# A graph convolution whose two edge streams begin with a chunk of 512 columns that stood near their end

## The chip, the cores and the metric

The kernel runs on one core of a Trainium2 chip. The metric is the device time of one execution in microseconds (us). The kernel before took 3414.15 us, the median of three runs (3410.12 to 3417.74). The core has five engines that run side by side and meet at semaphores: PE (TensorE, matrix products), DVE (VectorE), ACT (ScalarE), POOL (GpSimd, here the one that issues gathers) and SP (SyncE, here the one that issues most transfers).

## The reference

A graph network with 3125 nodes, 103125 directed edges (sorted by destination), 64 features and four layers. Each layer computes a softmax-weighted sum over the edges that end in a node:

```python
e   = edge_attr @ enc_edge_w + enc_edge_b
msg = relu(h[src] + e) + 1e-7
m   = msg * t
ex  = exp(m - segment_max(m, dst)[dst])
agg = segment_sum(msg * ex / segment_sum(ex, dst)[dst], dst)
z   = relu(layernorm((h + agg) @ w1 + b1)) @ w2 + b2
```

Between layers there is a residual sum and a layer norm with ReLU; after the last, the input is added and normalised.

## The kernel before, in words

**Streams and chunks.** The sorted edges are cut into two halves, and the second is reversed. Each half lies on 64 partitions (one for each feature) with the edges along the columns, 51712 columns in all (149 of them padding at the front). The columns are worked off in 54 chunks: 49 of 1024 (numbers 0 to 48), then 512, 512, 256, 128, 128. The first 128 columns of chunk 0 are padding and are not gathered. A running maximum, a running denominator and a running numerator go through the columns as scans (lines 938, 953, 969), so that the chunks of a stream must follow each other on DVE. `g = layer * 54 + c` counts the chunks over all layers.

**One chunk, engine by engine.**
- PE multiplies the edge attributes by the encoder (`edge_product`, line 547), into one of four PSUM tiles X. The product of chunk c + 2 is issued after the transposes of chunk c, and waits until the numerator scan of chunk c - 2 has released the tile.
- `h[src]` comes in two ways. POOL gathers rows of `z_table`, 128 edges with one indirect DMA (line 504), and PE transposes them onto X (`add_rows`, line 576). For a chosen chunk only the first 512 columns are gathered, and the second 512 are made on PE by 150 products with one-hot matrices (`add_by_one_hot`, line 566): 60 in part 0 and 90 in part 1, issued around the transposes of the chunks before.
- ACT makes the messages (lines 684, 686), four exponent steps (696 to 701) and the penalties of the next chunk from the bytes `keep` (674). DVE does the running maximum, then the numerator of the chunk before (`numerator_sums`), then the denominator of this one. DVE's first instruction of a chunk is line 936.
- SP stores the rows of each chunk in `rows_table` by four transfers (374), loads attributes (353) and `keep` (364; one block for two chunks, asked for at even chunk numbers, two slots).

**One-hot matrices.** 31 chunks are chosen: 0, 1, and those from 4 to 48 that are even or of the form 8n + 5. In layer 0 the matrices are built by DVE (1033) and ACT (713), used at once for the 29 chunks from 4 on, and stored; those of chunks 0 and 1 are built in slots 50 and 52, for later layers. In layers 1 to 3 they are loaded by ACT's queue (`load_part`, 739), 1.31 MB for part 0 and 1.97 MB for part 1, into two slots: part 0 of the chosen chunk k is used before the transposes of k - 1, and its slot is loaded again from ACT's place in chunk k - 1 (part 0) and k (part 1). Only layers 1 to 3 take chunks 0 and 1 by one-hot.

**Order at the start of a layer.** POOL's gathers wait for the last piece of `z_table`; PE's one-hot products wait for `z_split`, set by DVE's `split_z` (line 998). PE's order is edge products of chunks 0 and 1, then the whole one-hot sum of chunk 0, then the transposes of chunk 0, then the one-hot sum of chunk 1. POOL may be three chunks ahead of PE's transposes. In layer 0, POOL also gathers one piece of keys (line 486) after each of the chunks 1 to 25, and ACT counts it.

Of the kernel before, what the change touches and what calls it, by code (L numbers as in the profile page):

```python
# [4 lines left out]
P = 128  # L5
F = 64
# [6 lines left out]
HALVES = 2  # L13
CH = 1024
KT = CH // P
BANK = 512
SLOTS = 3
XS = 4
SQ = 32
NSQ = CH // SQ  # L20
FB = F // SQ
# [3 lines left out]
COLS = -(-EA // BANK) * BANK  # L25
NBLK = -(-COLS // CH)
TAIL = [512, 512, 256, 128, 128]
WIDTHS = [CH] * ((COLS - sum(TAIL)) // CH) + TAIL
STARTS = [sum(WIDTHS[:_c]) for _c in range(len(WIDTHS))]
NCH = len(WIDTHS)  # L30
# [25 lines left out]
FIRST_CHOSEN = [c for c in range(NCH) if (c % 2 == 0 or c % 8 == 5) and 4 <= c <= 48]  # L56
CHOSEN = [c for c in range(NCH) if c < 2 or (c % 2 == 0 or c % 8 == 5) and 4 <= c <= 48]
BUILD_SLOT = {0: 50, 1: 52}
# [10 lines left out]
def width(c):  # L69
    return WIDTHS[c]  # L70

# [39 lines left out]
def block_of(c):  # L111
    return STARTS[c] // CH, STARTS[c] % CH


def attr_place(c):
    blk, at = block_of(c)
    if width(c) == CH:
        return blk * P, 0, P
    return blk * P + at * HALVES // CH * F, at * HALVES % CH, F
# [19 lines left out]
def gnn_kernel(nc, x_nodes, x_t, dst_stream, src_tiles, src_banks, attr_t, enc_node_w, enc_node_b, enc_edge_w, enc_edge_b,  # L139
# [10 lines left out]
    rows_by_chunk = rows_table[0:BOUNDARY_ROW, :].rearrange("(c b i h) (f e) -> c (h f) i b e", c=NBLK, i=SQ, h=HALVES, f=FB)  # L150

    with ExitStack() as ctx:
# [180 lines left out]
        def _(sp):  # L333
# [33 lines left out]
            def store_rows(layer, c, parts):  # L367
                g = layer * NCH + c
                blk, at = block_of(c)
                b0 = at // SQ  # L370
                n = NSQ - b0 if layer == 0 and c == NCH - 1 else width(c) // SQ
                sp.wait_ge(rows_ready, g + 1)
                for a in parts:
                    sp.dma_start(rows_by_chunk[blk, a, :, b0:b0 + n, :],  # L374
                                 rows[g % 2][a * SQ:(a + 1) * SQ, 0:n].rearrange("i b q j -> i b (q j)")).then_inc(stored[g % 2], 16)
# [288 lines left out]
        def _(act):  # L664
# [122 lines left out]
            for layer in range(LAYERS):  # L787
# [33 lines left out]
                blk, at = block_of(c)  # L821
                b0 = at // SQ
                n = NSQ - b0 if layer == 0 else width(c) // SQ
                for a in range(NSTORE // 2, NSTORE):
                    act.dma_start(rows_by_chunk[blk, a, :, b0:b0 + n, :],
                                  rows[g % 2][a * SQ:(a + 1) * SQ, 0:n].rearrange("i b q j -> i b (q j)")).then_inc(stored[g % 2], 16)
# [438 lines left out]
```

## Time and profile before

| what | value |
|---|---|
| median of 3 runs | 3414.15 us |
| profiled execution, its own time | 3407.53 us |
| its span, first to last instruction | 3405.7 us |
| mean granted TensorE clock | 0.876 |
| DVE busy | 2874.5 us (84%) |
| POOL busy (0.3 us of issue before each gather not counted) | 2310.8 us (68%) |
| DMA, mean busy share of the 16 engines | 88.8% in queues q1, q10 and q0 together |

Layer 0's stream begins on DVE at 54 us, those of layers 1, 2 and 3 at 1020, 1819 and 2620 us. Between the last chunk of a layer and the first of the next lie the node stage and the start of the stream, 96 to 99 us. A row of the timeline gives start, duration, engine, line, operation, count, and in brackets how long the engine sat idle before and what released it.

### The profile page before, as it was taken

The numbers are of one execution on the slowest core, as the hardware profiler recorded it, in microseconds if no ns is written. First come the engines' busy times: TensorE is split into PE (matmuls) and PEld (weight loads), VectorE is DVE, ScalarE is ACT, GpSimd is POOL, SyncE is SP. The second block draws the span as 40 slices with busy tenths as digits, with TensorE's granted clock in tenths as the row PEclk, the third lists the DMA queues.
The fourth block names the chain that finished last, engine by engine and source line by source line (L and its number), as shares of the span: only waits on it lengthen the run. The fifth ranks groups of instructions, "written<-read, shape, count | busy, mean of one in ns | idle before, by whom it ended". The sixth has DMA issues, their size and how long they took to land.

```text
span 3405.7 us, 55091 instructions
## 1 busy us (share of the span) xinstructions
PE 2695.8 (79%) x21852; PEld 1361.5 (40%) x21852; DVE 2874.5 (84%) x2835; ACT 1782.3 (52%) x2240; POOL 2310.8 (68%) x2381
## 2 busy tenths in 40 slices
PE   2778877888279888988748899889938988899854
PEld 1334333334144444444333444444415444444423
DVE  6899999999857888898976888888875889888895
ACT  2777775666424544455443544545543445444554
POOL 5777776676257777777627777777735777777742
PEclk9889988889669999999858999999957999999975
DMA  5999999999838999999847999999964999999971
GB/s 147 282 273 311 304 289 259 272 289 287 231 117 269 287 304 302 295 295 297 215 122 219 305 292 306 283 298 309 276 154 136 294 292 294 305 298 300 280 187 39
DMA packets 1047266, 878.26 MB, mean 258 GB/s; under 512 B 911066, under 2 KB 937183, under 8 KB 1015200
## 3 DMA queue, kind: packets, MB, share of 16 engines
q1 hardware_dynamic: 940912, 478.76, 54.8%
q10 hardware_dynamic: 28960, 305.28, 23.8%
q0 software_dynamic: 77136, 90.71, 10.2%
q8 instruction: 171, 2.80, 0.3%
q14 instruction: 87, 0.71, 0.1%
HBM read 555.79 MB, written 318.70 MB: 257 GB/s over the span
## 4 chain that ended last, share of the span: by engine, by line
DVE 34%; PE 16%; SPq 15%; issue 9%; POOL 9%; DMA 8%; ACT 8%; DVEq 0%; ACTq 0%; POOLq 0%
PE X L566 13%; SPq L374 9%; POOL gath L504 8%; DVE decay L938 7%; DMA keep<-keep_dram 6%; DVE state_all L969 6%; DVE one_hot L1033 5%; DVE rows_all L924 4%; SPq L364 4%; DVE X L943 4%; DVE state_all L953 3%; ACT X L686 2%; ACT msg L684 2%; SPq L353 1%; PE X L547 1%
## 5 line engine op out<-in xcount | busy, mean ns | idle before, releaser
L504 POOL DMA_INDIRECT gath<-z_table,idx x2248 | 2189.6, 974 | 862.5 <-issue 694.3
L566 PE MATMUL X<-one_hot,z_parts 128*64 128x512 fp8e5 x11550 | 1352.1, 396 | 149.2 <-DVE one_hot L1033 124.5
L566 PEld LDWEIGHTS X<-one_hot,z_parts 128*64 128x64 bf16 x11550 | 666.9, 114 | 870.8 <-DVE one_hot L1033 162.3
L566 PE MATMUL X<-between,z_parts 128*64 128x512 fp8e5 x6750 | 763.2, 386 | 2.8 <-DMA between<-one_hot_dram 2.8
L696 ACT ACTIVATE decay<-X 128x1024 f32<-128x1024 f32 (+2 forms) x216 | 209.3, 969 | 927.5 <-DVE X L943 923.2
L566 PEld LDWEIGHTS X<-between,z_parts 128*64 128x64 bf16 x6750 | 380.8, 112 | 394.6 <-issue 72.1
L924 DVE STREAM_TRANSPOSE rows_all<-state_all 128x1024 f32<-128x1024 f32 (+3 forms) x432 | 505.9, 1171 | 8.4 <-DMA rows_table<-rows_all 1.0
L547 PE MATMUL X<-attr,enc_edge 64*64 64x512 f32 (+1 forms) x1648 | 268.5, 703 | 306.8 <-DVE state_all L969 297.4
L953 DVE TENSOR_TENSOR_SCAN state_all<-decay,state_all,X 128x1024 f32<-128x1024 f32 (+2 forms) x216 | 468.2, 2168 | 20.0 <-ACT X L701 20.0
L938 DVE TENSOR_TENSOR_SCAN decay<-X,decay 128x1023 f32<-128x1023 f32 (+2 forms) x216 | 477.2, 2209 | 7.7
L969 DVE TENSOR_TENSOR_SCAN state_all<-decay,state_all,X 128x1024 f32<-128x1024 f32 (+2 forms) x216 | 468.1, 2167 | 0.0
L684 ACT ACTIVATE msg<-X,edge_bias 128x1024 f32<-128x1024 f32 (+2 forms) x216 | 226.1, 1047 | 278.2 <-PE X L576 278.2
L936 DVE TENSOR_TENSOR decay<-decay,top 128x1 f32<-128x1 f32 x216 | 34.2, 158 | 351.7 <-ACT X L686 338.0
L674 ACT ACTIVATE decay<-keep 128x1024 f32<-128x1024 uint8 (+2 forms) x216 | 213.7, 990 | 223.4 <-DMA keep<-keep_dram 223.4
L956 DVE SCALAR_TENSOR_TENSOR X<-msg,X 128x1024 f32<-128x1024 f32 (+2 forms) x216 | 250.4, 1159 | 7.5
L943 DVE TENSOR_TENSOR X<-X,decay 128x1024 f32<-128x1024 f32 (+2 forms) x216 | 250.0, 1157 | 0.0
L576 PE MATMUL X<-ident,gath 128*128 128x128 f32 x1128 | 180.9, 296 | 80.9 <-DMA gath<-z_table,idx 80.7
L686 ACT ACTIVATE X<-msg,tcol 128x1024 f32<-128x1024 f32 (+2 forms) x216 | 229.6, 1063 | 7.0
L519 POOL DMA_INDIRECT between<-rows_table,pos_i x100 | 95.0, 950 | 180.3 <-DMA rows_table<-ends_row 104.4
L699 ACT ACTIVATE decay<-decay 128x1024 f32<-128x1024 f32 (+2 forms) x216 | 213.1, 987 | 0.0
L697 ACT ACTIVATE X<-X 128x1024 f32<-128x1024 f32 (+2 forms) x216 | 208.1, 963 | 0.0
L701 ACT ACTIVATE X<-X 128x1024 f32<-128x1024 f32 (+2 forms) x216 | 207.1, 959 | 0.0
(160 smaller groups left out, 1458.0 us busy)
## 6 DMA issues: line engine op xcount, KB each, us to landing
rows_table<-rows_all SPq DMA_DIRECT2D x784, 256.0 KB
attr<-attr_t SPq DMA_DIRECT2D x196, 512.0 KB
one_hot<-one_hot_dram ACTq DMA_DIRECT2D x48, 1920.0 KB
between<-one_hot_dram ACTq DMA_DIRECT2D x45, 1920.0 KB
one_hot<-one_hot_dram ACTq DMA_DIRECT2D x48, 1280.0 KB
one_hot_dram<-one_hot SPq DMA_DIRECT2D x31, 1920.0 KB
between<-one_hot_dram ACTq DMA_DIRECT2D x45, 1280.0 KB
one_hot_dram<-one_hot SPq DMA_DIRECT2D x31, 1280.0 KB
```

Source lines behind the costliest of these rows:

```text
L374: sp.dma_start(rows_by_chunk[blk, a, :, b0:b0 + n, :], rows[g % 2][a * SQ:(a + 1) * SQ, 0:n].rearrange("i b q j -> i b (q j)")).then_inc(s ...
L504: pool.indirect_dma_start(out=gath[s][:, n * F:(n + 1) * F], out_offset=None, in_=z_table, in_offset=bass.IndirectOffsetOnAxis(ap=idx[:, c ...
L547: last = nc.tensor.matmul(X[g % XS][h * F:(h + 1) * F, b * BANK:b * BANK + w], enc_edge2[b * F:(b + 1) * F, :], attr[s][b * F:(b + 1) * F, ...
L566: last = nc.tensor.matmul(x[h * F:(h + 1) * F, BANK:CH], z_parts[:, i * GB + k, third, :], bank[:, i, k, h * BANK:(h + 1) * BANK], start=F ...
L684: nc.scalar.activation(msg[s][:, 0:w], X[g % XS][:, 0:w], ACT.Relu, bias=edge_bias[:, :]).then_inc(msg_ready, 1)
L686: nc.scalar.activation(X[g % XS][:, 0:w], msg[s][:, 0:w], ACT.Copy, scale=tcol[:, layer:layer + 1])\
L924: v.transpose(rows[g % 2][:, 0:w // SQ, q, :], state[g % 2][:, q, 0:w].rearrange("p (b j) -> p b j", j=SQ))\
L938: v.tensor_tensor_scan(out=m[:, 1:w], data0=x[:, 0:w - 1], data1=m[:, 1:w], initial=m[:, 0:1], op0=ALU.max, op1=ALU.add).then_inc(run_max, 1)
L943: v.tensor_tensor(x, x, m, ALU.subtract).then_inc(shifted, 1)
L953: v.tensor_tensor_scan(out=state[g % 2][:, 0, 0:w], data0=decay[s][:, 0:w], data1=X[g % XS][:, 0:w], initial=state[(g - 1) % 2][:, 0, befo ...
L956: v.scalar_tensor_tensor(out=X[g % XS][:, 0:w], in0=msg[s][:, 0:w], scalar=EPS_MSG, in1=X[g % XS][:, 0:w], op0=ALU.add, op1=ALU.mult).then ...
L969: v.tensor_tensor_scan(out=state[g % 2][:, 1, 0:w], data0=decay[s][:, 0:w], data1=X[g % XS][:, 0:w], initial=state[(g - 1) % 2][:, 1, befo ...
```

## The change

The widths become 512, then 49 times 1024, then 512, 256, 128, 128: still 54 chunks and the same columns. Chunk 0 has 512 columns and no one-hot part in any layer. The chosen chunks become 1, 2, and those from 5 to 49 that are odd or of the form 8n + 6; the two that only later layers use are built in slots 51 and 53. The chunks of 1024 keep their order of chosen and not chosen, each with a number higher by one. What goes by the number itself does not move: `keep` is asked for at even numbers (its first block is now 1536 columns), keys are gathered after chunks 1 to 25, and `load_part` has its place by rules on c. Since a chunk no longer lies within one block of 1024, rows are stored by squares of 32 columns at the same addresses as before, and each chunk's attributes get rows of their own.

```diff
-TAIL = [512, 512, 256, 128, 128]
-WIDTHS = [CH] * ((COLS - sum(TAIL)) // CH) + TAIL
+HEAD = [512]
+TAIL = [512, 256, 128, 128]
+WIDTHS = HEAD + [CH] * ((COLS - sum(HEAD + TAIL)) // CH) + TAIL
...
-FIRST_CHOSEN = [c for c in range(NCH) if (c % 2 == 0 or c % 8 == 5) and 4 <= c <= 48]
-CHOSEN = [c for c in range(NCH) if c < 2 or (c % 2 == 0 or c % 8 == 5) and 4 <= c <= 48]
-BUILD_SLOT = {0: 50, 1: 52}
+FIRST_CHOSEN = [c for c in range(NCH) if (c % 2 == 1 or c % 8 == 6) and 5 <= c <= 49]
+CHOSEN = [1, 2] + FIRST_CHOSEN
+BUILD_SLOT = {1: 51, 2: 53}
...
-def block_of(c):
-    return STARTS[c] // CH, STARTS[c] % CH
+ATTR_PARTS = [P if w > BANK else F for w in WIDTHS]
...
 def attr_place(c):
-    blk, at = block_of(c)
-    if width(c) == CH:
-        return blk * P, 0, P
-    return blk * P + at * HALVES // CH * F, at * HALVES % CH, F
+    return sum(ATTR_PARTS[:c]), 0, ATTR_PARTS[c]
...
-    rows_by_chunk = rows_table[0:BOUNDARY_ROW, :].rearrange("(c b i h) (f e) -> c (h f) i b e", c=NBLK, i=SQ, h=HALVES, f=FB)
+    rows_by_square = rows_table[0:BOUNDARY_ROW, :].rearrange("(b i h) (f e) -> (h f) i b e", i=SQ, h=HALVES, f=FB)
...
-                b0 = at // SQ
-                n = NSQ - b0 if layer == 0 and c == NCH - 1 else width(c) // SQ
+                b0 = STARTS[c] // SQ
+                n = NBLK * NSQ - b0 if layer == 0 and c == NCH - 1 else width(c) // SQ
...
-                    sp.dma_start(rows_by_chunk[blk, a, :, b0:b0 + n, :],
+                    sp.dma_start(rows_by_square[a, :, b0:b0 + n, :],
```

PE at the start of layer 1 (after the node stage), before: the products of two chunks, then all 150 one-hot products of chunk 0 ahead of its transposes (x4), then the 150 of chunk 1.

```order
L547 MATMUL X<-attr,enc_edge 64x512 x8
L566 MATMUL X<-one_hot,z_parts 64x512 x150
L576 MATMUL X<-ident,gath 128x128 x4
L566 MATMUL X<-between,z_parts 64x512 x150
L547 MATMUL X<-attr,enc_edge 64x512 x4
L576 MATMUL X<-ident,gath 128x128 x4
L547 MATMUL X<-attr,enc_edge 64x512 x4
L576 MATMUL X<-ident,gath 128x128 x8
L547 MATMUL X<-attr,enc_edge 64x512 x4
L566 MATMUL X<-one_hot,z_parts 64x512 x60
L576 MATMUL X<-ident,gath 128x128 x8
L566 MATMUL X<-one_hot,z_parts 64x512 x90
```

The same place in the changed kernel (its line numbers are 4 lower):

```order
L543 MATMUL X<-attr,enc_edge 64x512 x6
L572 MATMUL X<-ident,gath 128x128 x4
L562 MATMUL X<-one_hot,z_parts 64x512 x150
L543 MATMUL X<-attr,enc_edge 64x512 x4
L562 MATMUL X<-between,z_parts 64x512 x60
L572 MATMUL X<-ident,gath 128x128 x4
L562 MATMUL X<-between,z_parts 64x512 x90
L543 MATMUL X<-attr,enc_edge 64x512 x4
L572 MATMUL X<-ident,gath 128x128 x4
L543 MATMUL X<-attr,enc_edge 64x512 x4
L572 MATMUL X<-ident,gath 128x128 x8
L543 MATMUL X<-attr,enc_edge 64x512 x4
```

Chunk 0's transposes now stand ahead of all one-hot products. Between the transposes of chunks 0 and 1 stand 150 + 60 one-hot products where 150 stood, since chunk 2 is chosen too.

ACT at the start of layer 1 (loads of one-hot matrices; 128x2560 is part 0, 128x3840 part 1), before:

```order
L674 ACTIVATE decay<-keep 128x1024
L739 DMA between<-one_hot_dram 128x2560
L739 DMA between<-one_hot_dram 128x3840
L684 ACTIVATE msg<-X,edge_bias 128x1024
L686 ACTIVATE X<-msg,tcol 128x1024
L739 DMA one_hot<-one_hot_dram 128x2560
L739 DMA one_hot<-one_hot_dram 128x3840
L696 ACTIVATE decay<-X 128x1024
L697 ACTIVATE X<-X 128x1024
```

And in the changed kernel:

```order
L670 ACTIVATE decay<-keep 128x512
L735 DMA between<-one_hot_dram 128x2560
L735 DMA between<-one_hot_dram 128x3840
L680 ACTIVATE msg<-X,edge_bias 128x512
L682 ACTIVATE X<-msg,tcol 128x512
L692 ACTIVATE decay<-X 128x512
L693 ACTIVATE X<-X 128x512
L695 ACT_TABLE_LOAD
L695 ACTIVATE decay<-decay 128x512
L697 ACTIVATE X<-X 128x512
L670 ACTIVATE decay<-keep 128x1024
L680 ACTIVATE msg<-X,edge_bias 128x1024
```

The third matrix is no longer loaded within chunk 0; its load stands behind the messages of chunk 1.

## Rows read from the trace of the kernel before

**Rows 1.** Waits of all engines: engine line, released by: us, times, longest

```profile
DVE decay L936 <- ACT X L686: 338.0, 96, 22.3
...
ACT decay L674 <- DMA keep<-keep_dram: 223.4, 67, 7.6
...
POOL between L519 <- DMA rows_table<-rows_all: 46.6, 1, 46.6
```

**Rows 2.** Windows of 20 us, layer 1: PE, PEld, DVE, ACT, POOL busy; PEclk, DMA share, GB/s

```profile
990.00:1010.00 20.00, 12.29 (x94) 5.74 (x92) 7.91 (x5) 0.00 (x0) 14.82 (x14) 0.68 0.72 252
...
1210.00:1230.00 20.00, 20.00 (x180) 9.98 (x178) 19.79 (x16) 12.93 (x14) 15.09 (x16) 1.00 1.05 348
```

**Rows 3.** Timeline of PE at the start of layer 1

```profile
998.10 18.72 PE L566 MATMUL X<-one_hot,z_parts 128*64 128x512 fp8e5 x150 [7.71 <-DVE z_parts L998]
...
1034.67 0.66 PE L576 MATMUL X<-ident,gath 128*128 128x128 f32 x4
...
1045.18 1.99 PE L547 MATMUL X<-attr,enc_edge 64*64 64x512 f32 x8 [7.81 <-DVE state_all L969]
1047.09 8.41 PE L566 MATMUL X<-one_hot,z_parts 128*64 128x512 fp8e5 x60
1055.44 1.09 PE L576 MATMUL X<-ident,gath 128*128 128x128 f32 x8
1066.29 1.09 PE L547 MATMUL X<-attr,enc_edge 64*64 64x512 f32 x8
1067.31 6.67 PE L566 MATMUL X<-between,z_parts 128*64 128x512 fp8e5 x60
```

**Rows 4.** Timeline of POOL, layer 1: gathers number 1, 6 and 46

```profile
991.22 0.94 POOL L504 DMA_INDIRECT gath<-z_table,idx  x1 [27.58 <-DMA z_table<-z_sb]
...
999.16 0.95 POOL L504 DMA_INDIRECT gath<-z_table,idx  x1 [0.30 <-issue]
...
1050.48 0.94 POOL L504 DMA_INDIRECT gath<-z_table,idx  x1 [0.30 <-issue]
```

**Rows 5.** Timeline of DVE, layer 1: first instructions of chunks 0, 1, 2, 4, 22 and 44

```profile
1019.75 0.16 DVE L936 TENSOR_TENSOR decay<-decay,top 128x1 f32<-128x1 f32 x1 [21.70 <-ACT X L686]
...
1037.72 0.16 DVE L936 TENSOR_TENSOR decay<-decay,top 128x1 f32<-128x1 f32 x1 [3.35 <-issue]
...
1049.71 0.15 DVE L936 TENSOR_TENSOR decay<-decay,top 128x1 f32<-128x1 f32 x1
...
1076.90 0.16 DVE L936 TENSOR_TENSOR decay<-decay,top 128x1 f32<-128x1 f32 x1 [3.07 <-ACT X L686]
...
1333.01 0.16 DVE L936 TENSOR_TENSOR decay<-decay,top 128x1 f32<-128x1 f32 x1 [6.23 <-ACT X L686]
...
1633.35 0.16 DVE L936 TENSOR_TENSOR decay<-decay,top 128x1 f32<-128x1 f32 x1 [1.67 <-ACT X L686]
```

**Rows 6.** Timeline of DVE, end of layer 1: first instructions of chunks 50 and 51

```profile
1708.17 0.15 DVE L936 TENSOR_TENSOR decay<-decay,top 128x1 f32<-128x1 f32 x1
...
1714.83 0.15 DVE L936 TENSOR_TENSOR decay<-decay,top 128x1 f32<-128x1 f32 x1
```

**Rows 7.** Timeline of POOL and PE, layer 0: last gather and transposes of chunks 0, 1

```profile
39.55 0.94 POOL L504 DMA_INDIRECT gath<-z_table,idx  x1 [0.30 <-issue]
42.04 1.97 PE L576 MATMUL X<-ident,gath 128*128 128x128 f32 x8 [10.74 <-DMA gath<-z_table,idx]
...
63.11 0.94 POOL L504 DMA_INDIRECT gath<-z_table,idx  x1 [0.30 <-issue]
...
70.44 1.97 PE L576 MATMUL X<-ident,gath 128*128 128x128 f32 x8 [24.53 <-DMA gath<-z_table,idx]
```

**Rows 8.** Layer 0, start: last gathers of chunks 3 and 4; DVE's chunk 3

```profile
107.51 1.10 POOL L504 DMA_INDIRECT gath<-z_table,idx  x1 [0.30 <-issue]
...
119.37 0.94 POOL L504 DMA_INDIRECT gath<-z_table,idx  x1 [0.30 <-issue]
...
115.71 0.16 DVE L936 TENSOR_TENSOR decay<-decay,top 128x1 f32<-128x1 f32 x1 [3.71 <-ACT X L686]
```

**Rows 9.** Layer 0: DVE's first instruction of chunk 26

```profile
503.52 0.16 DVE L936 TENSOR_TENSOR decay<-decay,top 128x1 f32<-128x1 f32 x1 [1.28 <-ACT X L686]
```

More of the change, by code:

```diff
@@ L368, in store_rows @@
                 g = layer * NCH + c
-                blk, at = block_of(c)
-                b0 = at // SQ
-                n = NSQ - b0 if layer == 0 and c == NCH - 1 else width(c) // SQ
+                b0 = STARTS[c] // SQ
+                n = NBLK * NSQ - b0 if layer == 0 and c == NCH - 1 else width(c) // SQ
                 sp.wait_ge(rows_ready, g + 1)
                 for a in parts:
-                    sp.dma_start(rows_by_chunk[blk, a, :, b0:b0 + n, :],
+                    sp.dma_start(rows_by_square[a, :, b0:b0 + n, :],
                                  rows[g % 2][a * SQ:(a + 1) * SQ, 0:n].rearrange("i b q j -> i b (q j)")).then_inc(stored[g % 2], 16)
@@ L820, in _ @@
                 act.wait_ge(rows_ready, g + 1)
-                blk, at = block_of(c)
-                b0 = at // SQ
-                n = NSQ - b0 if layer == 0 else width(c) // SQ
+                b0 = STARTS[c] // SQ
+                n = NBLK * NSQ - b0 if layer == 0 else width(c) // SQ
                 for a in range(NSTORE // 2, NSTORE):
-                    act.dma_start(rows_by_chunk[blk, a, :, b0:b0 + n, :],
+                    act.dma_start(rows_by_square[a, :, b0:b0 + n, :],
                                   rows[g % 2][a * SQ:(a + 1) * SQ, 0:n].rearrange("i b q j -> i b (q j)")).then_inc(stored[g % 2], 16)
@@ L1218 @@
     src_s = chunked(streams(src, 0)).transpose(3, 1, 2, 0).reshape(P, NBLK * KT * HALVES)
-    src_b = np.stack([streams(src, 0)[:, c * CH + BANK:(c + 1) * CH] for c in BANKS]).reshape(P, SUB)
+    src_b = np.stack([streams(src, 0)[:, STARTS[c] + BANK:STARTS[c] + CH] for c in BANKS]).reshape(P, SUB)
     attr_h = streams(attr, 0)
-    attr_s = np.zeros((NBLK * P, CH), attr.dtype)
+    attr_s = np.zeros((sum(ATTR_PARTS), CH), attr.dtype)
     for c in range(NCH):
```

## The prediction, as it was put on record before the changed kernel ran

> **What bounds the kernel now.** I read the table of waits first, then DVE's timeline for the first instruction of every chunk (line 936), then PE and POOL at the places where those starts are late, then the windows for the DMA share.
>
> DVE is the engine through which all columns must go, and the profiled execution leaves it 338.0 us of idle time ahead of line 936 [rows 1]. Its chunk starts show three stages in each of the layers 1 to 3.
>
> - *Front.* The stream of layer 1 starts at 1019.75, after 21.70 us of idling [rows 5]: PE had put 150 one-hot products of chunk 0 (18.72 us) ahead of its transposes. Chunk 1 starts 18 us later, after 150 more. In that time POOL gathers without a pause, 1.25 us apart (from number 6 at 999.16 to number 46 at 1050.48, 40 steps in 51.3 us [rows 4]).
> - *Middle.* A chunk costs DVE 12.0 us of work (chunk 1 to 2, without a gap, 1037.72 to 1049.71), 96 for eight. But from chunk 4 (1076.90) to chunk 44 (1633.35) are 556.45 us [rows 5], 111.3 for eight chunks. Read the same way, layers 2 and 3 give 111.3 and 111.4. The DMA share is 1.05 in a window there, against 0.72 at the front [rows 2], so I take the transfers (rows out, one-hot matrices, `keep` in) as what paces the middle. Where a chunk is late, it is mostly an even one, whose `keep` bytes came late: 223.4 us of ACT's time in 67 waits [rows 1]; or one behind one-hot sums of neighbouring chosen chunks.
> - *Tail.* After the last loads DVE runs without a gap. The interval from chunk 50 to 51 (512 columns) is 1714.83 - 1708.17 = 6.66 us [rows 6].
>
> Layer 0 differs: until chunk 4 POOL's gathers bound it (DVE's chunk 3 waits 3.71 us [rows 8]), later DVE itself, which also builds matrices.
>
> **The method.** The full chunks keep their order, each with its number raised by one. So I set new chunk k + 1 against old chunk k. The change is then a delay of this pairing at the front, less one chunk of 512 at the tail. The work in all is the same: as many gathers, products and scans.
>
> **Layers 1 to 3, front.** New chunk 0 needs only six gathers. The sixth is issued at 999.16 [rows 4], and I take 4 us until it lands. The bounds for this: in layer 0 the transposes begin 42.04 - 39.55 = 2.5 us after the last gather of chunk 0, and 70.44 - 63.11 = 7.3 us after that of chunk 1, with loads under way [rows 7]; number 46 had landed at most 5.0 us after its issue (1050.48 against 1055.44) [rows 3, 4].
>
> The sum in times of layer 1:
> - landed 1003.2, transposes 0.7, then PE's 150 products of chunk 1 at 18.7 (first ones of the layer, as before), edge product 1.1, 60 products of chunk 2 at 6.7, transposes 0.7 [rows 3]: chunk 1 is ready at 1031.1.
> - DVE starts 2.4 us after the transposes end (1034.67 + 0.66 to 1037.72 [rows 3, 5]): new chunk 1 at 1033.5. Its cycle is about 11.6, as ACT's exponents are late behind a short numerator; PE's 90 products, 1.5 times 6.7, and what goes with them give the same: new chunk 2 at 1045.1.
> - The numerator that frees the tile for the edge product of new chunk 5 comes 7.5 us later (1037.72 to 1045.18 in the old pair), at 1052.6. The old one was at 1045.18 [rows 3]: a delay of 7.4.
> - Then PE does 2.0 + 8.4 us (1063.0) and needs number 54, issued 8 steps of 1.25 after 1050.48, at 1060.5, and landed at 1064.5. That is 1.5 more: 9 us.
>
> The early start of DVE, 1006 instead of 1020, thus buys only half a chunk. The next full chunk waits for PE, which now has 210 one-hot products between the first two transposes [PE's order above], and later for POOL, which has eight gathers more ahead of each paired chunk, 8 x 1.25 = 10 us. The delay is 5.9 with a landing of 2.5 us (no wait for number 54), and 12.6 with 7.3 (10.7, and then 1.9 at number 54).
>
> At a landing of 4 us it stands that the six gathers pass the 3.28 MB of one-hot matrices that ACT asks for at 998. In the Trainium skill (DMA: Bandwidth & Descriptors, Queues, rings and completion order) each DMA engine "round-robins between the queue rows it has work for", packet by packet, so that a small gather shares the engines with a big load and needn't wait for its end. The 5.0 us at most of number 46 agree, though its window was not full. By service in order of issue instead, it would land some 11 us after its issue (3.28 MB at about 300 GB/s, between the 252 and 348 of [rows 2]), and the delay would be 13 to 16. I keep 9.
>
> **Layers 1 to 3, middle.** Per eight chunks the bytes are the same, so the paired delay is carried through, if the DMA engines pace this stage. What does change is the phase: `keep` is still asked for at even numbers, and the chosen chunks are now odd. I cost this at nothing, since another order doesn't take work away from a full queue, and bound it by the two mechanisms below, -27 and +31 us in all.
>
> ACT loads the third matrix behind the messages of new chunk 1 (about 1034 instead of 1018.65 for old chunk 0). It is used at 1055; 1.31 + 1.31 MB at half of 300 GB/s take 17 us. Just in time; 2 us at worst, in the upper bound.
>
> **Layers 1 to 3, tail.** One interval of 6.66 us falls away [rows 6]. POOL has then only a few gathers left and is ahead of DVE, so that its own shift is hidden. Per layer 9 - 6.7 = +2.3 (from -0.8 to +5.9, and +8 with the late matrix); for three +7 (-2 to +24).
>
> **Layer 0.** Old chunk 3 waits for the gather issued at 107.51. New chunk 4 also needs eight gathers and a piece of keys more, those that end the stretch at 119.37 [rows 8]: +11.9, and DVE, which had waited 3.71, could not have been earlier by itself (new chunk 3 is bound by gathers in the same way). Chunk 0 doesn't matter, since the gathers after it bind. Back come 6.7 at the tail, where DVE is the bound (its matrix building moves along with its chunks), and 1.3 from old chunk 26, which waited for ACT's count of keys [rows 9]: the keys stop at number 25, one chunk earlier in the pairing. But the last built matrix is now stored within the last 400 columns; POOL waits here for the last rows (46.6 us in all, once [rows 1]), and 1.97 MB at 300 GB/s are 6.6 us, most of which overlaps. I take 1 of them. Together +5 (+3.9 to +10).
>
> The edits of addresses (attributes, squares) change neither counts nor sizes of transfers: nothing.
>
> **Sum.** 5 + 7 = +12. The profiled execution took 3407.53 us, 1.8 more than its span, and would take 3419.5. It lies 6.6 below the median of the runs shown, 3414.15; on the scale of the medians the forecast is 3426 us. Its own range, from +2 to +34 without the phase, is 3416 to 3448.
>
> **Rivals.**
> - *The phase helps (faster).* At each group of three neighbouring chosen chunks PE makes the second one late by about 6 us (6.7 + 10.0 for its products and 1.8 for the rest [rows 3], against 12.0). Its number is now even, so that the `keep` wait falls into the same gap. Before, it came one chunk later: chunk 22 waits 6.23 us [rows 5], and the six such chunks of a layer some 18. If half of it really goes, 9 us in each of three layers, -27 + 12 = -15: 3399. It decides once it gives back over 4 us a layer. Against it: the cycle of eight takes 111.3 in three layers alike, although its waits lie elsewhere each time.
> - *The phase hurts.* The load that runs beside the fetch of `keep` is now part 1, 1.97 MB, where it was part 0, 1.31: 0.66 MB at 300 GB/s, 2.2 us. With 19 plain even chunks in each of three layers and a quarter of it exposed, +31: 3457. For it speaks that `keep` is what ends most waits; against it again the full queues, and that the rows before it then go out faster.
> - *Front and tail cancel (no change).* The gathers land after 2.5 us, layer 0 stays at +4: in all about +2, 3416.
> - *Nothing lands in time.* First gathers behind the load, 13 to 16 of delay, +4 to +7 more a layer: 3438 to 3447, inside the range.
>
> **How the numbers follow.** The forecast with its own range gets 0.48, with its lowest part (under +6.8) counted as no change; the phase that helps 0.20, mostly faster; the phase that hurts 0.12; the cancelling 0.15; the late landing 0.05. About 0.2%, 6.8 us, is what a measurement of this kernel tells from no change. Slower: 0.12 + 0.05 + 0.40 of the forecast = 0.57. Same: 0.15 + 0.08 + 0.02 of the helping phase = 0.25. Faster: 0.18. The range reaches to both phases in part: 3402 to 3452. The likeliest case's own range stands above.
>
> **What would show it.** In the trace of the changed kernel, layer 1 counted from its first gather (991.2 before):
> - first instruction of DVE 15 us after it, not 28.5; chunk 1 at 42 (old chunk 0 at 28.5), chunk 5 at about 94.7 (old chunk 4 at 85.7). If chunk 5 comes at 91 or less, the front is cheaper than I say.
> - DVE without a gap from chunk 49 on, and 6.7 us less for it.
> - eight chunks of the middle in 111.3 us. Under 110 or over 112.5 the phase matters, and I am wrong about what paces it; the waits of ACT for `keep` say which way.
> - layer 0: chunk 4 at 127.6, not old chunk 3's 115.7, and the last chunk some 4 us later than before.
> - the same count of instructions, gathers and bytes. If not, the pairing fails.

## The result, and the profile after

| kernel | median | range | runs |
|---|---|---|---|
| before, beside it | 3412.3 us | 3410.1 to 3417.7 | 4 |
| changed | 3486.7 us | 3481.2 to 3492.5 | 4 |

The ratio is 1.0211 (95% interval 1.0189 to 1.0233): the change costs 74 us where +12 was forecast, and the time lies 35 us above the range. The profiled execution took 3490.05 us, 1.9 more than its span, against 3407.53: +82.5.

The table of waits of the changed kernel answers to [rows 1] (engine line, released by: total, times, longest):

```profile
DVE decay L931 <- ACT X L682: 369.1, 85, 10.5
ACT decay L670 <- DMA keep<-keep_dram: 361.8, 67, 10.8
...
POOL gath L500 <- PE X L572: 164.0, 75, 17.6
```

ACT still waits 67 times for `keep`, but 361.8 us where it was 223.4. POOL's line of the same table before was:

```profile
POOL gath L504 <- PE X L576: 90.4, 44, 12.8
```

The amount of work is unchanged, as the first lines of the page show (55091 instructions, DVE 2874.6 us busy as against 2874.5), with the same packets and bytes:

```profile
span 3488.2 us, 55091 instructions
...
DMA packets 1047266, 878.26 MB, mean 252 GB/s; under 512 B 911066, under 2 KB 937183, under 8 KB 1015200
```

The front of layer 1. POOL's first and sixth gather, PE's first transposes, and DVE's first instructions of chunks 0, 1, 2 and 5, from the timeline of the changed kernel (start, duration, engine, line), which answer to [rows 3 to 5]:

```profile
995.39 0.94 POOL L500 DMA_INDIRECT gath<-z_table,idx  x1 [27.43 <-DMA z_table<-z_sb]
...
1003.34 0.94 POOL L500 DMA_INDIRECT gath<-z_table,idx  x1 [0.30 <-issue]
...
1009.84 1.11 PE L572 MATMUL X<-ident,gath 128*128 128x128 f32 x4 [15.29 <-DMA gath<-z_table,idx]
```

```profile
1012.44 0.16 DVE L931 TENSOR_TENSOR decay<-decay,top 128x1 f32<-128x1 f32 x1 [10.22 <-ACT X L682]
1039.08 0.16 DVE L931 TENSOR_TENSOR decay<-decay,top 128x1 f32<-128x1 f32 x1 [16.91 <-issue]
1050.48 0.15 DVE L931 TENSOR_TENSOR decay<-decay,top 128x1 f32<-128x1 f32 x1
...
1090.87 0.16 DVE L931 TENSOR_TENSOR decay<-decay,top 128x1 f32<-128x1 f32 x1 [4.29 <-ACT X L682]
```

Chunk 5 starts 1090.87 - 995.39 = 95.5 us after the first gather. Old chunk 4 started after 85.7: the front costs 9.8 us, and 9 was forecast. In layers 2 and 3 it costs 9.9 and 8.5.

The middle of layer 1. DVE's first instructions of chunks 14 to 19 and of chunk 45:

```profile
1224.94 0.16 DVE L931 TENSOR_TENSOR decay<-decay,top 128x1 f32<-128x1 f32 x1 [9.19 <-ACT X L682]
1236.93 0.15 DVE L931 TENSOR_TENSOR decay<-decay,top 128x1 f32<-128x1 f32 x1
1254.73 0.16 DVE L931 TENSOR_TENSOR decay<-decay,top 128x1 f32<-128x1 f32 x1 [5.72 <-ACT X L682]
1266.73 0.18 DVE L931 TENSOR_TENSOR decay<-decay,top 128x1 f32<-128x1 f32 x1
1282.29 0.16 DVE L931 TENSOR_TENSOR decay<-decay,top 128x1 f32<-128x1 f32 x1 [3.45 <-ACT X L682]
1294.28 0.15 DVE L931 TENSOR_TENSOR decay<-decay,top 128x1 f32<-128x1 f32 x1
...
1671.70 0.15 DVE L931 TENSOR_TENSOR decay<-decay,top 128x1 f32<-128x1 f32 x1
```

Only every second chunk waits, and it is the even one, for which `keep` is fetched. From chunk 5 to 45 are 580.83 us, 116.2 for eight chunks; layers 2 and 3 give 115.0 and 115.9. Before it was 111.3, 111.3 and 111.4. The differences of 4.9, 3.7 and 4.5, five cycles in each layer, make 66 us. Read by the pairing of the prediction (new chunk k + 1 against old chunk k), the delay grows from 13.97 to 38.35 us between chunk 5 and chunk 45 of layer 1. With the chunks up to 49 the growth comes to 25, 20 and 25 us in the three layers, 70 in all.

The rest went much as forecast. The time from the start of the last full chunk of layer 1 (old 48, new 49) to that of the last chunk is 35.7 us before and 29.1 after: 6.6 back. Layer 0 ends 2.95 us later (DVE's last chunk at 923.35 instead of 920.40), and the next layer's first gather comes 995.39 - 991.22 = 4.2 later. The three fronts cost 28.3 us and the three tails give back 19.6; with the 4.2 and the 70 that makes 83, and 82.5 were measured.

How the fetch and the wait follow each other is seen on SP's queue and ACT, at the even chunk that starts at 1254.73. SP (SPq is its issuing of transfers), in the changed kernel:

```profile
1263.36 7.23 SPq L370 DMA_DIRECT2D rows_table<-rows_all  x4
1270.62 4.32 SPq L361 DMA_DIRECT2D keep<-keep_dram  x2
```

And ACT at that place:

```profile
1264.65 0.33 ACTq L735 DMA_DIRECT2D one_hot<-one_hot_dram  x1
...
1279.04 1.06 ACT L670 ACTIVATE decay<-keep 128x1024 f32<-128x1024 uint8 x1 [4.44 <-DMA keep<-keep_dram]
```

The same place before, old chunk 16, which started at 1246.77, on SP and on ACT:

```profile
1255.39 6.44 SPq L374 DMA_DIRECT2D rows_table<-rows_all  x4
1261.87 4.14 SPq L364 DMA_DIRECT2D keep<-keep_dram  x2
```

```profile
1256.69 0.33 ACTq L739 DMA_DIRECT2D between<-one_hot_dram  x1
...
1269.41 1.06 ACT L674 ACTIVATE decay<-keep 128x1024 f32<-128x1024 uint8 x1 [2.81 <-DMA keep<-keep_dram]
```

SP asks for `keep` behind four row stores, ACT has asked for a one-hot part 5 to 6 us earlier, and the penalties wait for `keep`. Both loads stand in ACT's place in chunk 17. In the changed kernel, where 17 is chosen, it is a part 1 (1.97 MB); before, where 18 is chosen, it was a part 0 (1.31 MB). Over the plain even chunks of layers 1 to 3 (those followed by one without a wait), `keep` is used 9.0 us after its request in the changed kernel and 7.7 before. The request itself comes 16.2 us after the start of the chunk instead of 15.2. The mean of all 63 pairs of chunks rose from 27.55 to 28.71 us, and 63 x 1.16 = 73 us.

### The profile page after: what moved, and what is told of

Same layout as the page of the kernel before. It is cut to its first block, busy times and chain, and to the rows that moved or that the text cites. A ratio compares the mean times of both kernels' runs of the same rounds, so it can differ in the third digit from the quotient of the medians.

```text
span 3488.2 us, 55091 instructions
## 1 busy us (share of the span) xinstructions
PE 2696.8 (77%) x21852; PEld 1361.6 (39%) x21852; DVE 2874.6 (82%) x2835; ACT 1781.7 (51%) x2240; POOL 2309.7 (66%) x2381
## 4 chain that ended last, share of the span: by engine, by line
DVE 34%; SPq 19%; DMA 10%; ACT 10%; issue 9%; PE 9%; POOL 9%; DVEq 0%; ACTq 0%; POOLq 0%
SPq L370 12%; POOL gath L500 9%; DVE decay L933 7%; DMA keep<-keep_dram 7%; PE X L562 7%; SPq L361 7%; DVE state_all L964 6%; DVE rows_all L919 5%; DVE one_hot L1028 5%; DVE X L938 4%; DVE state_all L948 2%; ACT X L682 2%; ACT msg L680 2%; ACT x_sb L709 1%; ACT between L709 1%
## 5 line engine op out<-in xcount | busy, mean ns | idle before, releaser
L670 ACT ACTIVATE decay<-keep 128x1024 f32<-128x1024 uint8 (+2 forms) x216 | 213.8, 990 | 361.9 <-DMA keep<-keep_dram 361.8
L680 ACT ACTIVATE msg<-X,edge_bias 128x1024 f32<-128x1024 f32 (+2 forms) x216 | 226.0, 1046 | 204.0 <-PE X L572 203.9
L515 POOL DMA_INDIRECT between<-rows_table,pos_i x100 | 95.1, 951 | 203.0 <-DMA rows_table<-ends_row 120.8
L572 PEld LDWEIGHTS X<-ident,gath 128*128 128x128 f32 x1128 | 127.0, 147 | 247.4 <-DMA gath<-z_table,idx 146.0
L543 PEld LDWEIGHTS X<-attr,enc_edge 64*64 64x64 f32 x1648 | 52.8, 149 | 428.6 <-issue 407.0
```

The costliest lines, as they stand in the source:

```text
L543: last = nc.tensor.matmul(X[g % XS][h * F:(h + 1) * F, b * BANK:b * BANK + w], enc_edge2[b * F:(b + 1) * F, :], attr[s][b * F:(b + 1) * F, ...
L572: last = nc.tensor.matmul(X[g % XS][:, k * P:(k + 1) * P], gath[s][:, k * P:(k + 1) * P], ident[:, :], is_transpose=True, start=False, sto ...
L680: nc.scalar.activation(msg[s][:, 0:w], X[g % XS][:, 0:w], ACT.Relu, bias=edge_bias[:, :]).then_inc(msg_ready, 1)
```

## The experiments

The theory after the result: the lost 70 us are the wait for `keep`, which the move by one number has set beside the larger part. The place of the request for `keep` in the pattern of chosen and unchosen chunks is called its phase here. The rival is that the DMA queues as a whole are the pace and `keep` only shows it. Each time is set against runs of the kernel before on the same chip; intervals are of 95%.

### The phase of `keep`, and `keep` out of the way

In `a_keep_odd` and `b_keep_odd` the blocks of `keep` begin at odd chunk numbers, in the changed kernel and in the one before. That gives the changed kernel the old neighbourhood back, and the old kernel the new one. (The first block is a single chunk then, NKEEP is 26 in both, and a block is asked for at the first chunk of the block before.)

```diff
-    return min(c // KEEP_CHUNKS, NKEEP - 1)
+    return min((c + 1) // KEEP_CHUNKS, NKEEP - 1)
...
-    return range(b * KEEP_CHUNKS, (b + 1) * KEEP_CHUNKS if b < NKEEP - 1 else NCH)
+    return range(max(b * KEEP_CHUNKS - 1, 0), (b + 1) * KEEP_CHUNKS - 1 if b < NKEEP - 1 else NCH)
...
```

> The changed kernel, with the keep blocks moved by one chunk: block 0 is chunk 0 alone, then chunks (1,2), (3,4) and so on, so that keep is asked for at odd numbers, in the same place against the chosen chunks as before the change. Theory P (the phase of keep against the chosen chunks cost the 70 us of the middle): the cycle of eight goes back from 115.7 to 111.4 us, ACT's waits for keep from 362 to about 225 us, and the time to about 3425 (3415 to 3435), what the prediction had without the phase. Rival W (the first chunk of 512 and the order of one-hot loads at the front disturb the stream, and keep is only where it shows): the time stays within 15 us of 3487.

> The kernel before, with the same move of the keep blocks: asked for at odd numbers while the chosen chunks are even. Theory P: it becomes slower by what the changed kernel lost in the middle, to about 3480 (3465 to 3495), cycle of eight 115 to 116, all of DVE's waits at odd numbers. Rival W: no more than 15 us slower.

In `a_keep3` and `b_keep3` there are three slots, and each block is asked for one block earlier.

```diff
-KEEP_SLOTS = 2
+KEEP_SLOTS = 3
...
```

> The changed kernel with three slots for keep, each block asked for two chunks (some 27 us) earlier. Theory P: no wait for keep is left (under 40 us of ACT's time), and the middle falls at least to 111.4 per eight chunks: 3425 or less. If the DMA engines pace the middle, as the prediction had it, the cycle then stays at 111 to 112 and other waits take the place; if keep's way (rows stored, keep issued, landed) paced it, the cycle falls to what PE allows, about 100 to 104, and the time to 3370 or less.

> The kernel before with three slots for keep. If the DMA engines paced its middle (prediction): within 10 us of 3412, cycle 111. If it was paced by keep: the cycle falls to 100 to 105 and the time to 3310 to 3370.

Measured, beside 3415.4 us of the kernel before:

| run | median | ratio (interval) | eight chunks, layers 1, 2, 3 | ACT waits for `keep` |
|---|---|---|---|---|
| a_keep_odd | 3442.8 | 1.0084 (1.0062 to 1.0106) | 112.3, 112.8, 113.1 | 262.7 |
| b_keep_odd | 3476.1 | 1.0183 (1.0162 to 1.0204) | 114.9, 114.6, 116.3 | 368.7 |
| a_keep3 | 3413.3 | 0.9987 (0.9973 to 1.0000) | 110.4, 110.8, 110.8 | 3.8 |
| b_keep3 | 3398.7 | 0.9948 (0.9928 to 0.9968) | 111.1, 110.3, 111.1 | 4.0 |

The kernel before, with nothing changed but the phase, loses 61 us and waits for `keep` as long as the changed one. The changed kernel, with the phase put back, recovers 47 of its 74 us: 27.4 us are left against the runs beside it. That is less than expected (3415 to 3435 us, a cycle of 111.4), and what the other part is was not tested. With a third slot the wait is gone, and the two kernels have the same cycle, 110.3 to 111.1 us. So the phase of `keep` is the cause of the loss in the middle. What remains of the change is 3413.3 - 3398.7 = 14.6 us, where the prediction had +12 for front, tail and layer 0. The two traces show it there: 6.8 us at layer 1's first gather (996.71 against 989.96), 26.1 lost at the three fronts, 19.5 given back at the three tails, and in the middle no more than 1.5 us, in sum over the three layers. `b_keep3` fell between its two expectations: the cycle stayed at 111, but the time is 17 us lower.

### What paces the middle without the wait

Both runs start from `b_keep3`. In `b_k3_gath14`, POOL makes 14 gathers instead of 16 for each full unchosen chunk of layers 1 to 3 (its loop runs to `issued_tiles`), so that the last 128 columns of such a chunk lack `h[src]` in both streams. In `b_k3_halfhot`, the loads of one-hot matrices bring only 64 of the 128 partitions from the third chosen chunk of a layer on, and the rest keeps older values.

```diff
+def issued_tiles(layer, c):
+    n = gathered_tiles(layer, c)
+    return n - 1 if layer > 0 and n == KT else n
...
-                    for n in range(first_tile(c) * HALVES, gathered_tiles(layer, c) * HALVES):
+                    for n in range(first_tile(c) * HALVES, issued_tiles(layer, c) * HALVES):
```

> The kernel before with three keep slots, and 14 instead of 16 gathers for each full chunk that isn't chosen, in layers 1 to 3 (the last 128 columns of both halves keep old data). Eight chunks then need 82 gathers and not 88. Theory G (with keep out of the way, POOL's gathers, one each 1.25 us, pace the middle: 88 x 1.249 = 109.9, measured 110.3 to 111.1): the cycle falls to 103 to 104.5, layers 1 to 3 get 35 to 45 us shorter each, the time about 3280 (3265 to 3305). Theory D (the DMA engines pace it, as the prediction said): the gathers are a tenth of the DMA time, 6 of 88 of them under 1% of it, so the cycle stays over 109 and the time over 3380.

```diff
-                act.dma_start(hot[j % HOT_SLOTS][:, a:b].bitcast(f32), one_hot_dram[n * P:(n + 1) * P, a:b].bitcast(f32))\
+                full = P if j < HOT_SLOTS else P // 2
+                act.dma_start(hot[j % HOT_SLOTS][0:full, a:b].bitcast(f32), one_hot_dram[n * P:n * P + full, a:b].bitcast(f32))\
```

> The kernel before with three keep slots, and only half of the bytes (64 of 128 partitions) of each one-hot load from the third on in layers 1 to 3; the other half keeps old data, all instructions stay. Theory G: cycle 110 as before, within 0.5 us (POOL's 88 gathers), time within 12 us of 3399. Theory D: 2 x 31 loads carry 23% of the DMA time, half of it goes, the cycle falls by 10 or more to what DVE and PE allow, 100, and the time to 3300 or less.

Measured, beside 3418.9 us of the kernel before: `b_k3_gath14` 3350.9 us, ratio 0.9797 (0.9775 to 0.9820), eight chunks in 108.5, 107.9 and 107.2 us; `b_k3_halfhot` 3404.5 us, ratio 0.9955 (0.9941 to 0.9970), eight chunks in 110.7, 111.0 and 111.3.

Two windows of 400 us in layers 1 and 2 show both (columns as in [rows 2]). First `b_keep3`:

```profile
1100.00:1500.00 400.00, 360.73 (x3038) 176.44 (x3036) 350.50 (x265) 206.05 (x208) 302.23 (x321) 0.94 1.02 300
1900.00:2300.00 400.00, 355.44 (x3038) 175.18 (x3036) 349.45 (x265) 205.59 (x207) 302.45 (x321) 0.96 1.02 300
```

Then `b_k3_halfhot`:

```profile
1100.00:1500.00 400.00, 362.25 (x3062) 176.33 (x3058) 350.47 (x267) 205.74 (x208) 302.31 (x321) 0.94 1.02 226
1900.00:2300.00 400.00, 360.46 (x3052) 176.17 (x3050) 351.05 (x267) 207.42 (x209) 302.47 (x321) 0.95 1.01 226
```

A quarter less data per second doesn't shorten the time or the cycle, and leaves the busy share of the DMA engines as it was: they aren't the pace. POOL is, with 321 gathers in 400 us in each row, 1.246 us from one to the next. A cycle of eight chunks has 88 gathers, and 88 x 1.249 = 109.9 us, against 110.3 to 111.1 measured. In `b_k3_gath14` a cycle has 6 gathers fewer (three of eight chunks are unchosen), and it falls by 3 us and not by the 7.5 that POOL alone would give. I had expected 3265 to 3305 us, so the next limit is nearer than I thought. The waits of this run name it. DVE's waits before its chunks fall from 13.7 us a cycle in `b_keep3` to 7.4, and another one comes up:

```profile
DVE rows_all L929 <- DMA rows_table<-rows_all: 67.3, 30, 7.4
```

DVE waits there until rows of an earlier chunk have been stored. In `b_keep3` this took 5.4 us in all; here it is 4.4 us in each cycle of eight. So the stores of rows, which are DMA, stand close behind POOL.

The changed kernel has POOL waiting instead, as its windows show:

```profile
1100.00:1500.00 400.00, 342.02 (x2924) 166.71 (x2922) 322.15 (x244) 189.07 (x191) 294.79 (x314) 0.93 0.97 284
1900.00:2300.00 400.00, 359.62 (x3078) 175.67 (x3076) 330.48 (x252) 192.46 (x194) 296.80 (x315) 0.94 0.99 289
```

And the kernel before in the same windows:

```profile
1100.00:1500.00 400.00, 355.25 (x3044) 173.52 (x3042) 344.45 (x262) 201.38 (x203) 302.15 (x322) 0.95 1.02 298
1900.00:2300.00 400.00, 358.89 (x3042) 174.59 (x3040) 343.64 (x261) 200.63 (x202) 302.45 (x321) 0.94 1.00 296
```

POOL's 321 or 322 gathers are its full pace. Before, the waits for `keep` were nearly hidden under it (a cycle of 111.3 us against 109.9); in the changed kernel they aren't any more.

### How much of the phase is the size of the part beside `keep`

`SPLIT = 3` cuts the one-hot matrices the other way round: part 0 has 1.97 MB, part 1 has 1.31.

```diff
-SPLIT = 2
+SPLIT = 3
```

> The kernel before with the one-hot parts cut 3 + 2 and not 2 + 3 pieces: part 0 is then 1.97 MB and part 1 1.31 MB, so that the larger part is loaded beside the fetch of keep, as in the changed kernel, with all chunk numbers and sizes as before. Theory S (the size of the part beside the keep fetch makes the phase dear): slower by 30 to 70 us, cycle 113.5 to 116, ACT's waits for keep over 300 us. Rival R (it is not the load's size, but where the row stores and the PE waits of the neighbouring chosen chunks fall against keep): within 15 us of 3415, keep waits 200 to 250.

> The changed kernel with the same cut, 3 + 2 pieces: the smaller part, 1.31 MB, now loads beside the fetch of keep. Theory S: most of the loss of the middle comes back, 3425 to 3450, cycle 111.5 to 113, keep waits under 280 us. Rival R: within 15 us of 3487.

> The kernel before with keep asked for at odd numbers and the one-hot parts cut 3 + 2: both changes together, so that the smaller part loads beside the keep fetch again. If the size of that part explains the whole of the phase: back to 3410 to 3425, cycle 111.5. If it explains a part, as the two cuts so far suggest (b_split3 37 us slower, a_split3 14 faster): 3440 to 3465, cycle 113 to 114.

`b_split3` took 3455.9 us beside 3418.9, ratio 1.0101 (1.0076 to 1.0126); `a_split3` 3473.1, ratio 1.0146 (1.0115 to 1.0176); `b_odd_split3`, which has the odd blocks too, 3437.7, ratio 1.0059 (1.0036 to 1.0082), beside 3417.1. On the kernel before this makes a square of differences (us) from the runs beside each:

| `keep` asked for in | smaller part beside it | larger part beside it | the size (other cut) alone |
|---|---|---|---|
| a chosen chunk (as before) | 0 | +37 | +37 |
| an unchosen chunk (as after) | +21 | +61 | +40 |
| this neighbourhood alone | +21 | +24 | |

Each entry has an interval of some 8 us either way. Within it the two causes add up, and the size of the neighbouring load is the larger one. The spans of the traces, one execution of each, give +50, +64 and +27 instead, so that the adding up isn't shown more closely than that. The other cut also sets 90 products ahead of the transposes where 60 stood. On the kernel before this isn't what costs: in a cycle of eight, ACT's waits for `keep` grow from 12.9 to 16.8 us and DVE's before its chunks from 14.9 to 18.8, while ACT's waits for PE stay (6.8 and 6.4). Over the whole kernel ACT waits 279.1 us for `keep` in `b_split3`, where I had expected over 300. `b_odd_split3` came out 2 us below the 3440 to 3465 expected for a part of the phase.

The landing of `keep` moves with the size: it is used 7.7 us after its request before and 9.6 in `b_split3`; 9.0 in `b_keep_odd` and 8.0 in `b_odd_split3`. The cause of the other 21 to 24 us is not shown. The trace says where they are: in `b_odd_split3` DVE's waits before the first two chunks of a group of three neighbouring chosen ones are 9.6 us a cycle instead of 7.5, and before the other six chunks 7.2 instead of 7.4.

On the changed kernel the same cut gives back only 14 us (20 against the runs beside each), by cycles of 113.1 to 114.7 instead of 115.0 to 116.2. This lies in the band of the rival, not in that of the theory (3425 to 3450). Its waits are:

```profile
ACT msg L680 <- PE X L572: 359.9, 65, 21.6
...
ACT decay L670 <- DMA keep<-keep_dram: 213.2, 61, 7.8
```

The wait for `keep` is below that of the kernel before (223.4 us), so here it isn't what is left of the loss; ACT waits 359.9 us for PE, where it was 203.9 in the changed kernel. The shorter cycles are worth 29 us, but the three fronts lose 17.6: chunk 5 comes 101.3, 100.3 and 101.3 us after the first gather, instead of 95.5, 94.7 and 95.1. Between the first two transposes stand 240 one-hot products there, where 210 stood.

### `keep` ahead of the row stores

The same two slots, but SP asks for the next block just before it stores the rows of the odd chunk, not after (and at chunk 0 of the later layers).

```diff
-                    if c % KEEP_CHUNKS == 0 and c // KEEP_CHUNKS < NKEEP - 1 and layer * NKEEP + c // KEEP_CHUNKS >= 1:
-                        load_keep(layer * NKEEP + c // KEEP_CHUNKS + KEEP_SLOTS - 1)
+                    if c == 0 and layer > 0:
+                        load_keep(layer * NKEEP + KEEP_SLOTS - 1)
...
+                    if (c + 1) % KEEP_CHUNKS == 0 and (c + 1) // KEEP_CHUNKS < NKEEP - 1:
+                        load_keep(layer * NKEEP + (c + 1) // KEEP_CHUNKS + KEEP_SLOTS - 1)
                     store_rows(layer, c, range(FB))
```

> The changed kernel with two keep slots, but SP asks for keep ahead of the four row stores it stood behind. Theory Q (what makes keep late is its place in SP's queue: it starts some 16 us after the chunk's start, behind the rows of the chunk before, and lands 9 us later): ACT's waits for keep fall below 80 us, the cycle to 110.5 to 111.5 (POOL's gathers), the time to 3405 to 3425, as with three slots. If the row stores only take its place in the queue and come late themselves: over 3440, with DVE waiting for stored rows.

> The kernel before with the same move of the request. Theory Q: 3395 to 3405, as with three slots, so that the two kernels are again 10 to 16 us apart (the front's price less the tail's return).

Beside 3417.1 us: `a_keep_early` 3416.2, ratio 0.9997 (0.9983 to 1.0011); `b_keep_early` 3398.1, ratio 0.9938 (0.9915 to 0.9961). ACT waits 22.3 and 16.2 us for `keep`, and the cycles are 110.1 to 110.8 in both. This is SP in `a_keep_early`:

```profile
1254.64 1.10 SPq L361 DMA_DIRECT2D keep<-keep_dram  x2
1255.79 11.11 SPq L370 DMA_DIRECT2D rows_table<-rows_all  x4
```

And ACT, whose penalties have no wait in brackets:

```profile
1266.55 1.04 ACT L672 ACTIVATE decay<-keep 128x1024 f32<-128x1024 uint8 x1
```

The two requests take 1.10 us to issue here, against 4.32 behind the stores. As a mean over layers 1 to 3 it is 1.6 us, against 4.1 before and 4.9 in the changed kernel. The stores behind them take longer in return (1.94 us each as a mean, 1.50 in the changed kernel), but DVE waits only 7.2 us in all for stored rows. With the same bytes and the same slots, the order on SP's queue alone takes the wait away: `keep` is late because it stands behind the rows. This makes the fastest kernel of the study, without a further slot, level with `b_keep3`, and 0.6% faster than the kernel before. `a_keep_early` and `b_keep_early` both fell into what was expected.

### What the last 15 us are

`a_even` has the changed widths with the chosen chunks at their old numbers, one place earlier in the pairing. POOL then has eight gathers fewer ahead of each paired chunk.

```diff
-FIRST_CHOSEN = [c for c in range(NCH) if (c % 2 == 1 or c % 8 == 6) and 5 <= c <= 49]
+FIRST_CHOSEN = [c for c in range(NCH) if (c % 2 == 0 or c % 8 == 5) and 4 <= c <= 48]
...
-BUILD_SLOT = {1: 51, 2: 53}
+BUILD_SLOT = {1: 50, 2: 52}
```

> The changed widths (512 first) with the chosen chunks at their old numbers (even or 8n + 5, from 4 to 48, and 1 and 2), so that the phase against keep is restored by moving the chosen chunks and not keep. Theory P: cycle 111.3 to 112.8 and keep waits of 220 to 270 us as in a_keep_odd; the time 3420 to 3450. If the loss lay in the sizes and not in the phase: over 3465.

It took 3422.7 us, ratio 1.0012 (0.9996 to 1.0027): no difference from the kernel before can be told. Its cycles are 112.8, 111.4 and 111.1, and ACT waits 246.4 us for `keep`. It differs from `a_keep_odd` (3442.8, the same neighbourhood of `keep`) by POOL's lead and by the place of the pattern. The traces put 8.4 us of the difference into layer 0, where the first gather of layer 1 comes at 987.45 us instead of 995.85, and the rest into the layers behind it. This speaks for the lead as what costs, also in the middle, but doesn't separate it.

`a_even_early` puts the edit of `a_keep_early` on top of it, to find out whether the 15 to 18 us between the two kernels are POOL's lead or PE's order at the front. The same program was measured three times, once with `b_keep_early` beside it (`b_keep_early2`).

> The changed kernel with the chosen chunks at their old numbers (1, 2, and from 4 on the even ones or of the form 8n + 5) and keep asked for ahead of the row stores. Without waits for keep the middle goes at POOL's pace, and the changed kernel was still 18 us behind the old one (3416.2 against 3398.1). Theory (POOL's lead): what is left is the eight gathers, 8 x 1.25 = 10 us, that POOL makes more than before ahead of each paired full chunk; with the chosen chunks one number earlier in the pairing these eight are gone, and each of the four layers gives back 3 to 6 us: 3392 to 3404, cycle of eight still 110 to 111. Rival (front on PE): what is left is the 210 one-hot products between the first two transposes and the ready times behind them; the pattern doesn't touch that, and the time stays at 3412 to 3420.

> The same kernel as a_even_early once more (its first run, and the kernel before beside it, took 4585 and 4615 us, which is another pace of the whole chip than in all other runs). Lead theory: 3392 to 3404, cycle of eight 110 to 111. Rival, the front on PE: 3412 to 3420.

> The kernel before with keep asked for ahead of the row stores, again, on the same chip as a_even_early2, so that the two can be set side by side: 3396 to 3400. Lead theory: within 5 us of a_even_early2. Rival: 14 or more under it.

> The same kernel as a_even_early once more, hoping for the pace of the first twelve runs. If the kernel before takes about 3415 beside it: lead theory (POOL's eight gathers are what is left), ratio 0.993 to 0.997 (3392 to 3404), cycle of eight 110 to 111. Rival, the front on PE: ratio 0.999 to 1.002 (3412 to 3420). If the kernel before again takes some 4600, the question stays open.

In all these runs every kernel took a third longer, the kernel before too: 4614.9, 4618.0 and 4695.0 us. The runs gave 4585.4 (ratio 0.9935, 0.9913 to 0.9956), 4591.3 (0.9943, 0.9927 to 0.9960) and 4686.7 (0.9981, 0.9965 to 0.9998); `b_keep_early2` 4614.2 (0.9983, 0.9968 to 0.9998), 23 us above `a_even_early2` beside it, which neither theory had expected. The waits of the first of them show that another engine is the bound there:

```profile
PEld X L564 <- issue: 1380.9, 2030, 5.9
DVE decay L933 <- ACT X L684: 1190.9, 155, 22.5
...
POOL gath L502 <- PE X L574: 945.7, 119, 19.4
```

POOL waits 945.7 us for PE, and PE has long stretches of "issue", in which nothing in the profile holds it. POOL's lead can decide nothing there, so these four runs say nothing on the question at the usual pace, and it stays open.

## Why the prediction was wrong

**The direction and the parts outside the middle were right.** The front was put at 9 us and cost 9.8 in layer 1 (9.9 and 8.5 in the others), with chunk 5 at 95.5 us after the first gather instead of 94.7. The gathers landed 6.5 us after the issue of the sixth (1003.34 to 1009.84), not 4, near the upper of my two bounds; that made chunk 0 start at 17.1 us and not 15. By my own sum it should have delayed chunk 5 by 11.4 us in all, so that the 9 came out in part by luck. The sum has a slip too: PE's time and the landing of number 54 move together, so its 1.5 us stay at every landing, and the bounds are 7.4 and 12.2, not 5.9 and 12.6. Neither matters against what was missed. The tail gave back 6.6 of the 6.66 forecast. In layer 0, chunk 4 came at 126.69 (forecast 127.6), and 4.2 us were left at the next layer's first gather (forecast 5). With the wait for `keep` out of the way in both kernels, the change costs 14.6 us (third slot) or 18.1 (earlier request), where the sum said 12.

**The step that failed is the phase of `keep`,** "I cost this at nothing, since another order doesn't take work away from a full queue". It cost 70 us of 82.5 in the two profiled executions, and 60 of 74 by the medians (74.4 less the 14.6 that are left with a third slot). Two things were wrong in it.

- *The pace of the middle was taken from a busy share.* A DMA share of 1.05 [rows 2] was read as a full queue. `b_k3_halfhot` moves 226 GB/s instead of 300 at the same share of 1.02 and in the same time. The pace was POOL's chain of gathers, 88 x 1.249 = 109.9 us for eight chunks. The row for it stood in front of me: 16 gathers in 20 us in the window 1210 to 1230 of [rows 2] is 1.25 us for each, POOL without a pause. The page hides it, since it counts 0.94 us of each gather as busy and gives POOL 68%.
- *So the wait for `keep` wasn't bound to a pace that would absorb it.* It was nearly hidden under POOL's pace (a cycle of 111.3 against 110.3 to 111.1 without it), and a lengthening came out almost in full: 3.9 us more of it in a cycle made the cycle 3.4 longer (`b_split3`). The rival "the phase hurts" had the right mechanism, the larger load beside the fetch. But I priced it with a quarter exposed, +31. Measured are 37 to 40 us for the other cut and 21 to 24 for the rest of the phase on the kernel before, and 70 in the changed one. Near full exposure (57 chunks x 2.2 us = 125 us at most) should have been the upper end. Moreover the stage from which `keep` is late is SP's queue, four stores ahead of it, and I didn't look there.

**The other rivals.** "The phase helps" was false in its sign: PE's wait and that for `keep` do fall on the same chunk now (even chunks wait 94.7 us in the five cycles of layer 1, odd ones 0.3; before 50.8 and 23.5), but their sum grew. Front and tail don't cancel: they leave 28.3 - 19.6 = 8.7 us in the three layers. A late landing of the first gathers was not seen; 6.5 us is less than the 11 that service in order of issue would give.

**My own test pointed the right way.** I had written that over 112.5 us for eight chunks the phase matters and I am wrong about what paces the middle. It came out at 115.0 to 116.2.

## What to carry to other kernels

A renumbering that leaves all work as it was can still move a small, urgent transfer beside a larger one, or behind other requests on its queue. Before it is costed at nothing, look for the wait nearest to the critical path that ends on a transfer, and see which requests stand ahead of it on the issuing engine and which loads run beside it; the cheap cure is to ask for it before the bulk stores. And find the pace of a stage by counting an engine's steps in a window, intervals between them included, not from its busy share, nor from that of the DMA engines.

## What the runs showed of the hardware

- The busy share of the DMA engines said little here of how near they were to a limit: 300 GB/s (`b_keep3`) and 226 GB/s (`b_k3_halfhot`) both showed 1.01 to 1.02, and the time was 3398.7 and 3404.5 us.
- Gathers of 128 rows followed each other on POOL at 1.249 us (0.94 and 0.30 of issue). In three kernels of unlike phase (before, `b_keep3`, `b_k3_halfhot`) it made 321 or 322 of them in 400 us.
- The two requests of `keep` took 1.6 us to issue on SP as a mean (1.10 in the row shown, 5.5 at most) ahead of a chunk's four row stores, and 4.1 to 4.9 us as a mean, 11.3 at most, behind them. The stores took 1.94 us each behind `keep` and 1.50 ahead of it.
- The sixth gather of layer 1 landed in 6.5 us or less beside 3.28 MB of one-hot loads asked for 0.6 to 1.0 us before it, where service in order of issue would give some 11 (an estimate, at 300 GB/s). The Trainium skill (DMA: Bandwidth & Descriptors, Queues, rings and completion order) has the engines take turns between the queues; the number agrees with that rather than with service in order of issue.
- The kernel before took 3412 to 3419 us in most runs and 4615 to 4695 us beside the last four. In `a_even_early` 637.0 us of PE's idle time at the one-hot products are put down to "issue", PE is busy for 3299.6 us (2700.7 in `a_keep_early`), and the mean granted clock is 0.796 (0.872). What brings this pace about isn't shown: the record has one chip number, 13, with both. Runs of the two paces can't be compared.
